# Graph network kernel, adjacency counts: one product of 200 columns for a tile becomes two of 100 on halves of the array's rows

## The reference, cut to what matters

```python
src = jnp.concatenate([_s, _d, _loop]); dst = jnp.concatenate([_d, _s, _loop])

def _mean_aggregate(x, src, dst, num_nodes):
    summed = jax.ops.segment_sum(x[src], dst, num_segments=num_nodes)
    deg = jax.ops.segment_sum(jnp.ones((src.shape[0],), x.dtype), dst, num_segments=num_nodes)
    return summed / jnp.maximum(deg, 1.0)[:, None]

h = jax.nn.relu(_sage_conv(x, src, dst, W1_l, b1, W1_r))
return _sage_conv(h, src, dst, W2_l, b2, W2_r)
```

## Time and profile before

| | |
|---|---|
| median of 3 runs | 8911.31 us |
| lowest and highest of them | 8875.33 and 8933.79 us |
| the profiled execution, its own time | 8838.25 us |
| its span, first to last instruction | 8835.3 us |

### The profile page before, as it was taken

One profiled execution on the slowest core, in us unless ns is written; L12 is line 12 of the kernel. 1 busy time (PEld: TensorE's weight loads), 2 busy tenths in 40 slices (PEclk: granted clock), 3 DMA queues, 4 the chain that ended last, 5 costly groups with the idle time before them and its releaser, 6 DMA issues. The chain is left out here.

```text
span 8835.3 us, 94325 instructions
## 1 busy us (share of the span) xinstructions
PE 5190.5 (59%) x31067; PEld 3677.3 (42%) x31067; DVE 4063.1 (46%) x8022; ACT 1650.5 (19%) x2811; POOL 4537.0 (51%) x4319
## 2 busy tenths in 40 slices
PE   4333333866366666666664546898887346445544
PEld 4333333645355555555543323444444224333333
DVE  6454444779444444444442213565555234433343
ACT  1111110148323232322321000000000112111111
POOL 3666664010355545555552243565553676777664
PEclk9999998679777777777776768899898667667676
DMA  3222210023311111111684533111111111111175
GB/s 67 65 65 61 63 60 19 21 91 157 87 38 37 37 36 37 36 38 37 35 36 111 203 110 139 29 30 29 28 29 26 18 15 17 17 15 18 15 14 14
DMA packets 388446, 441.45 MB, mean 50 GB/s; under 512 B 241139, under 2 KB 312320, under 8 KB 387981
## 3 DMA queue, kind: packets, MB, share of 16 engines
q0 software_dynamic: 137696, 130.26, 14.4%
q1 hardware_dynamic: 191113, 286.63, 10.1%
q10 hardware_dynamic: 59568, 23.69, 1.2%
HBM read 358.46 MB, written 82.34 MB: 50 GB/s over the span
## 5 line engine op out<-in xcount | busy, mean ns | idle before, releaser
L950 POOL DMA_INDIRECT at_far<-att_table,at_rec x1184 | 1268.2, 1071 | 1476.0 <-DVE p_spread L1351 714.8
L1507 POOL DMA_INDIRECT p_far<-table,p_rec x1184 | 1322.0, 1117 | 652.9 <-issue 357.8
L2137 PE MATMUL g_l_ps_sum<-g_l_row,g_l_of 128*128 128x400 f32 x3224 | 1192.3, 526 | 195.4 <-issue 170.2
L2067 POOL DMA_INDIRECT g_l_got<-table,g_l_index x806 | 805.7, 1000 | 551.6 <-DVE g_l_index L2075 308.3
L1405 PE MATMUL p_ps_outer<-p_spread,p_basis 128*25 128x40 f32 (+1 forms) x4736 | 834.5, 355 | 384.0 <-issue 236.3
L533 POOL DMA_INDIRECT rec_r<-so_r_rec,so_r_place x806 | 814.0, 1010 | 455.4 <-issue 232.1
L2137 PEld LDWEIGHTS g_l_ps_sum<-g_l_row,g_l_of 128*128 128x128 f32 x3224 | 638.9, 199 | 749.3 <-issue 301.8
L1405 PEld LDWEIGHTS p_ps_outer<-p_spread,p_basis 128*25 128x25 f32 (+1 forms) x4736 | 669.9, 190 | 554.1 <-issue 377.7
L488 PE MATMUL so_r_look<-so_r_table,so_r_lo_t 128*128 128x26 f32 x1612 | 425.1, 434 | 787.5 <-DVE so_r_table L432 745.9
L2079 DVE TENSOR_SCALAR g_l_row<-g_l_iota,edge_row 128x800 f32<-128x800 f32 x806 | 485.3, 676 | 575.3 <-remote 417.5
L488 PEld LDWEIGHTS so_r_look<-so_r_table,so_r_lo_t 128*128 128x128 f32 x1612 | 417.5, 356 | 796.8 <-DVE so_r_table L432 570.9
(11 more groups left out here) (456 smaller groups left out, 5907.8 us busy)
## 6 DMA issues: line engine op xcount, KB each, us to landing
adjacent<-ad_by_chunk SPq DMA_DIRECT2D x74, 800.0 KB, 3.3
so_r_row<-pad_src SPq DMA_DIRECT2D x62, 832.0 KB
g_l_counts<-adjacent SPq DMA_DIRECT2D x60, 800.0 KB
g_l1d_counts<-adjacent SPq DMA_DIRECT2D x59, 800.0 KB
so_r_low<-pad_lo_src SPq DMA_DIRECT2D x62, 416.0 KB
at_far<-att_table,at_rec POOLq DMA_INDIRECT x1184
p_far<-table,p_rec POOLq DMA_INDIRECT x1184
rec_r<-so_r_rec,so_r_place POOLq DMA_INDIRECT x806
```

The costliest lines, as they stand in the source:

```text
L950: pool.indirect_dma_start(out=far[b][:, t, :], out_offset=None, in_=g.att_table[:, :], in_offset=bass.IndirectOffsetOnAxis(ap=rec[b][:, t, ...
L1507: pool.indirect_dma_start(out=sl.far[b][:, t, :], out_offset=None, in_=table[:, :], in_offset=bass.IndirectOffsetOnAxis(ap=sl.rec[b][:, t, ...
L2067: pool.indirect_dma_start(out=got[b][:, j, :], out_offset=None, in_=table[:, :], in_offset=bass.IndirectOffsetOnAxis(ap=index[b][:, j:j + ...
L2137: last = nc.tensor.matmul(ps_sum[k][:], of4[b][:, j, :, :].rearrange("p k f -> p (k f)"), row1[b][:, j, k * COLS:(k + 1) * COLS], start=Fa ...
```

## The change

Each tile is split into its two halves of 64 slots, which are 4 chunks each. A slot's cell is now the block times 4 plus the chunk within its half, so `cell1` has 100 columns for a tile in place of 200 (`cells_of`). For that the stage makes `quarter`, the partition's chunk number less 4 in the upper half, with two instructions on one column. PE makes a matmul for each half, over the half's 64 partitions: 32 in a group in place of 16, with the lower and the upper half in turn. In PSUM a set has its lower halves in one bank and its upper halves in the other. ACT's cast reads the 800 counts of a set from both banks and writes them to the same places as before, in runs of 4 in place of 8. The rest of the stage and the numbers in `adjacent` are the same.

```diff
+    HALF, CH = 2, o.per_tile // 2
+    cells_of = NB * CH
...
-        digits, cells = sb("digits", [P, P, GROUP], BF16), sb("cells", [P, HI], BF16)
+        digits, cells = sb("digits", [P, P, GROUP], BF16), sb("cells", [P, cells_of], BF16)
         node_f = sb("node_f", [P, groups], F32)
+        upper, quarter = sb("upper", [P, 1], F32), sb("quarter", [P, 1], F32)
         lo1 = [sb(f"lo1{b}", [P, P, GROUP], BF16) for b in two]
-        cell1 = [sb(f"cell1{b}", [P, GROUP, HI], BF16) for b in two]
+        cell1 = [sb(f"cell1{b}", [P, GROUP, cells_of], BF16) for b in two]
...
-        ps_set = [c.enter_context(nc.psum_tensor(f"ad_ps_set{k}", [P, SET, 256], F32)) for k in two]
+        ps_set = [c.enter_context(nc.psum_tensor(f"ad_ps_set{k}", [P, HALF, SET, P], F32)) for k in two]
...
-                ch.put(nc.vector.tensor_copy(cells[:], iota_i[:]))
+                ch.put(nc.vector.tensor_copy(cells[:], iota_i[:, 0:cells_of]))
+
+                ch.step(nc.vector.tensor_scalar(upper[:], g.sixteenth[:], float(CH), float(CH), ALU.is_ge, ALU.mult))
+                ch.put(nc.vector.tensor_sub(quarter[:], g.sixteenth[:], upper[:]))
...
-                ch.step(nc.vector.tensor_scalar(cell[:], part_i[:], float(o.per_tile), g.sixteenth[:], ALU.mult, ALU.add))
+                ch.step(nc.vector.tensor_scalar(cell[:], part_i[:], float(CH), quarter[:], ALU.mult, ALU.add))
...
-                        for j in range(SET):
-                            last = nc.tensor.matmul(ps_set[k % 2][:, j, 0:HI], lo1[b][:, :, k * SET + j], cell1[b][:, k * SET + j, :],
-                                                    start=True, stop=True)
+
+                        for m in range(SET * HALF):
+                            r = m % HALF
+                            j = m // HALF
+                            rows = slice(r * (P // HALF), (r + 1) * (P // HALF))
+                            last = nc.tensor.matmul(ps_set[k % 2][:, r, j, 0:cells_of], lo1[b][rows, :, k * SET + j],
+                                                    cell1[b][rows, k * SET + j, :], start=True, stop=True)
...
-                        nc.scalar.copy(counts[b][:, :, cols].rearrange("p k (j c) -> p j k c", c=o.per_tile),
-                                       ps_set[k % 2][:, :, 0:HI].rearrange("p j (k c) -> p j k c", c=o.per_tile)).then_inc(taken, 1)
+                        nc.scalar.copy(counts[b][:, :, cols].rearrange("p k (j r c) -> p r j k c", r=HALF, c=CH),
+                                       ps_set[k % 2][:, :, :, 0:cells_of].rearrange("p r j (k c) -> p r j k c", c=CH)).then_inc(taken, 1)
```

## The result

| | before | after |
|---|---|---|
| median, runs | 8889.89 us, 20 | 8938.18 us, 20 |
| lowest to highest | 8820.69 to 8956.43 | 8868.37 to 9006.41 |
| ratio | | 1.0045 (1.0026 to 1.0065) |
| the profiled execution | 8838.25 us | 8979.86 us |
| adjacency stage in it | 418.2 us | 458.8 us |

The change makes the kernel slower, by 0.45%, which is 40 us. The two medians are 48 us apart; the ratio leaves out the one run of the changed kernel that was in its slow state (9006.41 us). I had forecast 28 us less. It is slower by less than 1%, but the sign was wrong, and the case that came true is rival 4, the clock, to which I gave 0.06.

What follows compares the result with a forecast made beforehand. DVE was taken to set the adjacency loop's 5.16 us period. Afterwards DVE's loop takes 4.75, ACT and PE's 4.71, together 4.76: 0.40 x 70 = 28 us saved, 8911 to 8883 us; range 8840 to 8938.

Steps and rivals of the forecast that it cites:

- rival 4: Adjacency loop: TensorE drops to 1.2 GHz throughout, period 6.26 us, 77 us lost, 8988 us; chance 0.06.
- DVE's part: Adjacency loop: cell one-hots of 100 columns cost 0.155 us each, not 0.181; DVE's period goes from 5.16 to 4.75.
- Rival 3: DVE: a narrow one-hot costs as much as a wide one, 0.181 us, so 8911 us; chance 0.09.
- ACT's part: The 296 casts of 800 elements, now in output runs of 4 instead of 8: taken to cost nothing more.
- Rival 5: ACT's casts pay for short runs: 0.72 us more on its loop, 19 us lost, 8930 us; chance 0.06.
- PE's part, the fourth set: Fourth set's products, now in pairs on two array halves, take 0.41 us against 0.40; ACT and PE loop 4.71.
- rivals 1 and 2: Fourth set: halves load one after the other, 8894 us, chance 0.17; or each load is dear, 8922 us, 0.04.
- "Against" in rival 4: Evidence that the clock stays: the histogram holds 1.00 with 26 columns per load, as does attention's 64-row stretch.
- clock above 0.9: Sign to look for in the profile after, should the forecast hold; a falling clock row would show rival 4.

Runs made afterwards that it cites:

- e1: Kernel before, with DVE writing only 100 of the 200 columns of each cell one-hot, PE as it was; period 4.756 us, stage 388.5 us.
- e6: Changed kernel with the second set's products issued three times and the third's twice, 56 a group; ratio 0.9951 against the kernel before, stage 394.7 us.
- e2: Changed kernel with 16 products over all 128 rows, 100 columns, in place of 32 over 64 rows; period 5.423 us, stage 434.3 us.
- e3: Changed kernel with each of the 32 products of 100 columns over all 128 rows, so no pairs; period 4.863 us, stage 398.6 us.
- e9: e3 with 26 columns in place of 100 in every second product, all loads over 128 rows; period 5.727 us, stage 458.6 us.
- e8: Changed kernel with both products of a pair on rows 0 to 63, none beside another; period 6.092 us, stage 486.0 us.
- e7: Changed kernel with only the second set's products issued twice, 40 a group; period 5.409 us, stage 434.0 us.
- e5: Changed kernel with each set's four lower halves issued before its four upper ones; ratio 1.0035 against the kernel before, stage 459.8 us.

## Why the prediction was wrong

By its own steps:

- **DVE's part: right.** A one-hot of 100 columns was put at 0.155; the starts in after are 0.155 apart, and DVE's loop is 4.76 in e1 and e6 (4.75 forecast). Rival 3 falls.
- **ACT's part: right.** Four casts in 3.04 us, as in the earlier trace rows; runs of 4 cost nothing. Rival 5 falls.
- **PE's part, the fourth set: right at full clock.** 0.41 was forecast. It is 0.39 in e6, and in after 0.49 cold and 0.38 warm (2089.96 to 2090.34). In after, the products' starts lie 3 to 6 ns apart within a pair, so the loads of the two halves don't take turns: rivals 1 and 2 fall. e2, with four unsplit products of 100 columns, has 0.29; the split thus costs 0.10 of the set, where I had 0.03 + 0.09.
- **The step that failed is "Against" in rival 4**, and with it the sum's unpriced premise of full clock ("clock above 0.9"): the 1.67 from the transposes to ACT's copy is 2.71 in the mean of after and 2.94 in a cold period, and it is 1.68 again in e1, e3 and e6 wherever the transposes are warm. The text against it was "the histogram holds 1.00 with 26 columns per load, and so does the 64-row stretch". The first half is void: the histogram lies where the trace has no record of the clock, and 130 to 1430 us, with PE busy for 36%, shows the same 1.00. (Nor does the spacing of 0.060 in the earlier trace rows tell the clock: in e9 one product of 100 columns and one of 26, each with its load, take 0.125 together at full clock and 0.126 at half. As the price of a pair it was right, 0.059 to 0.060 in after at full clock.) The second half is true and doesn't carry over: those 3 us have PE busy for 3.00 with fp32 products of 256 columns, while the adjacency loop has PE busy for 68% and products of 100. And the 0.97 of the earlier trace rows told that the loop was at full clock, not with how much to spare. By e2, halving the products' columns in it is enough to lose it.
- **Rival 4's mechanism was right and its price too high**: 77 us against 40.6. Its cold period, 6.26, is measured as 6.06 (the set is 0.49, where I had added 0.24 to 0.41; the transposes 2.94 to the copy, where I had 2.98). But the rival had the loop cold all the time, while 63% of the time, and 76% of the distances between transposes, are cold: 5.778 a period in place of 6.26, and 0.61 x 70 = 43 us. It also said that 19 cold periods of 70 suffice to turn the sign, and both shares are well beyond that.
- **The median.** 8883 was carried from a median of 8911 of three runs; 20 runs of the same kernel have 8890. So 21 us of the distance to 8938 are scatter in the base, and the ratio, 1.0045 where 28 us less would be 0.9968, is the fair comparison. That 8938 lies so near the upper end of the range is chance: that end was made of scatter and rivals 1, 2, 3 and 5, none of which came true, and rival 4 was left out of it.

A better use of the profile as it was: the sum showed a gain of 28 us that a cold period in four would cancel, while the change took away half of the products' streaming in a loop in which PE was idle for a third of the time. The gain and the price stood in the text; the chance was wrong, since it rested on the two rows.

## What to carry to other kernels

Where a change makes PE's work smaller in a loop that PE doesn't bound, price the loop at half clock before the gain is counted, above all if another piece of PE's work (here 25 transposes) lies on a loop of waits. A row that shows full clock elsewhere is no evidence unless its stretch has clock records and a PE as lightly used. If the clock falls, repeating work in PE's idle time can be cheaper than the lost clock: here three extra sets a group turned a ratio of 1.0045 into 0.9951, and the stage from 458.8 to 394.7 us.

## What the runs showed that I had not expected

- PE busy for 88% of a stretch at a granted clock of 0.68 (e8, products over 64 rows on one half), and for 68% at 0.98 (before).
- Weight loads alone didn't hold the clock: e9 has those of e3 and fewer streamed columns, and 0.74 in place of 1.00.
- The profile's clock row is 1.00 for the first 1.46 ms and more of all eleven traces, where there is no clock record. In the kernel before, PE's spacing just ahead of the first record is that of half clock (67 ns; 36 at full).
- The clock does not simply fall and stay: in after, single periods run from 5.07 to 6.36, and with more PE work per period the mean goes up step by step, 0.69, 0.78 (e7) and 0.97 (e6).
- Products of the two halves that are issued four and four start side by side all the same (e5): within a set, the order of issue is not the order in which the halves start. That is read from the spacing of the starts and the length of the set, since a record doesn't tell which rows it used.
